# Block scale of an FP4 quantisation as a scalar_tensor_tensor with a constant column, and new slots for the jobs of a software pipeline

## The chip, the cores and the metric

One core of one Trainium2 chip. The metric is the device time of the whole program in microseconds (us), the median of three runs. "Profiled run" is one more execution, taken with the hardware profiler; its own time is given beside its span (first to last instruction).

## The reference

The input is 16 sequences of 1024 tokens, 256 wide, float32. A selective state space layer (a Mamba layer with 4 heads of 128 channels and 16 states per channel) is followed by a gated feed-forward layer whose activations and weights are quantised to FP4 and back, 16 values to a block:

```python
def fp4_quant_dequant(x):
    xb = x.reshape(shape[:-1] + (shape[-1] // 16, 16))
    scale = jnp.max(jnp.abs(xb), axis=-1, keepdims=True) / 6.0
    scale = jnp.maximum(scale, jnp.float32(1e-12))
    idx = jnp.searchsorted(_MID, jnp.abs(xb / scale))
    return (_GRID[idx] * jnp.sign(xb) * scale).reshape(shape)

# per head:  s = s * exp(d_t * A) + (d_t * u_t) * B_t ;  y_t = sum_n s[n] * C_t[n]
x = x + mamba(layernorm(x))
n = layernorm(x)
q = fp4_quant_dequant
x = x + q(silu(q(n) @ q(w_gate).T) * (q(n) @ q(w_up).T)) @ q(w_down).T
```

## The kernel before

The work is cut in two ways. A *unit* is one head of one chunk of 512 tokens: 128 units, eight to a sequence (the four heads of the early chunk, then the four of the late one). A *tile* is 128 tokens: 128 tiles as well. So one long loop over units carries one tile of the layer norm ("norm"), the preparation of one unit ("pre"), the scan of one unit ("scan") and one tile of the output projection and the feed-forward ("post"), each job of it at a different distance from the unit being scanned. A unit is cut into 16 steps, n = 0 to 15, one for each state.

**VectorE** is the backbone. In step n it first multiplies the B row of step n+1, which TensorE has spread over the partitions of a PSUM bank, with `du` (L970, "db"; not for n+1 = 1, 5, 9, 13, whose product GpSimd makes). Then comes what `between` holds for this step, then the scan of state n (L991, `tensor_tensor_scan` of 512 tokens), then what `behind` holds. In the units of a late chunk the scan starts from a carried column, in those of an early one from 0.0.

**GpSimd (POOL)** multiplies pairs of finished states with the C rows (`weigh`, L747, eight in a unit, each needs the scan of state 2p+1), makes four B products (`drive`, L738), and does the block multiplications of the quantisation (L757, L769, L786, L799), `du` (L795), the gate of y (L763) and the power -0.5 of both variances (`rstd`, L728), for which it waits for ScalarE's sum of squares of the post tile (L568). All of its operands lie in SBUF.

**ScalarE** makes the decays (L480) and evacuates and normalises; **TensorE** does all products; **SyncE** issues the DMAs of rows.

The order on each engine is written by hand as slots: `due("post", 22)` in `step` is true in step 22 mod 16 = 6, for the tile that lies 22 // 16 units back. Within one step the jobs run in the order of the code. Each job waits on semaphores for the jobs that it needs, so the slots set the order of an engine and nothing else.

**The quantisation of an activation tile** on VectorE: `block_max` (L835), `block_scale` (L838: max times 1/6, then the maximum with 1e-12), `block_recip` (L841), and after GpSimd's and ScalarE's parts `step_up` and `step_down` (L895, L898). It is done twice for each tile: for the normalised activations (`vs`, 16 blocks, input `v2`) and for the hidden ones (`hs`, 44 blocks, input `hv`). `v_norm` on GpSimd (L769) needs `block_recip(vs)`, `h_norm` (L757) needs `block_recip(hs)`, `v_quant` (L799) needs the last `step_down` of v. The weights are quantised once at the start, with `block_scale` too and with larger steps of the same kind (L871, L845, L848, L851, L854), whose operands are all in SBUF.

The order within a unit before, as far as the argument needs it (step: jobs):

- VectorE: 0: x1 (L942); 6, before the scan: gated 0, round up h 0, block_max(v); 6, behind it: round down h 0, **block_scale(v)**, y (L937), recip(v); 7: round up h 1, gated 1, round down h 1; 8: v up, output tile (L927); 9: v down; 12: block_max(h); 14: **block_scale(h)**; 15: recip(h).
- GpSimd: 0: weigh 7 of the unit before, drive 5; 1: h_norm; 3: weigh 0, rstd; 4: weigh 1, weigh 2; 6: v_norm, drive 9; 8: drive 13; 9: gate of y; 10: h_quant, du, v_quant; 11: weigh 3; 12: weigh 4; 15: drive 1, weigh 5, weigh 6.
- ScalarE from the sum over x1 (L655) to the squares (L568): decay 6, xn, fetch h 1; decays 7, 8, mid, centred v; xnt, squares of norm (L558), decay 5, table and silu gate 0, squares of post (L568).

Of the kernel before, what the change touches and what calls it, by code (L numbers as in the profile page):

```python
# [18 lines left out]
P = 128  # L19
# [120 lines left out]
def build(nc, hidden, win_t, conv_w, conv_b, xw, dtw, dt_b, a_log, dskip, wo_t, w_gate, w_up, w_down,  # L140
# [4 lines left out]
    with ExitStack() as ctx:  # L145
# [13 lines left out]
        less = sb("less", [2, P], BF16)  # L159
        minus_half = sb("minus_half", [2])  # L160
# [198 lines left out]
        def _(sp):  # L359
# [42 lines left out]
            def step(b, j, n):  # L402
                u, due = timetable(b, j, n)
                if w := due("scan", 1):
                    spread_c(w, 2)
                if w := due("scan", 4):
                    copy_b(w, 13)
# [6 lines left out]
                if w := due("scan", 4):  # L414
                    spread_c(w, 3)
                if w := due("scan", 6):
                    spread_c(w, 4)
                if w := due("scan", 6):
                    spread_c(w, 5)
# [4 lines left out]
                if w := due("scan", 12):  # L424
                    spread_c(w, 7)
                if w := due("scan", -4):
                    copy_b(w, 5)
                if w := due("scan", 2):
                    copy_b(w, 9)
                if w := due("scan", 0):  # L430
                    spread_c(w, 1)
                if t := due("post", 0):
                    wait(sp, x1_done, t.val(plus=-1))
                    sp.dma_start(xres[:, t.mod(2), :], x_tiles[t.val()]).then_inc(ld_res[t.mod(2)], 16)
                if w := due("scan", -8):
                    copy_b(w, 1)
                if w := due("scan", 11):
                    spread_c(w, 6)
                if w := due("scan", -3):
                    spread_c(w, 0)  # L440
                if t := due("post", 78):
                    sp.wait_ge(o_done, t.val(plus=1))
                    sp.dma_start(out_tiles[t.val()], ot[:, t.mod(2), :]).then_inc(ot_free[t.mod(2)], 16)

# [13 lines left out]
        def _(act):  # L458

            act.preload_act_table_set("exp_and_others")  # L460
            act.wait_ge(zeroed, 6)
# [47 lines left out]
            def step(b, j, n):  # L509
                u, due = timetable(b, j, n)  # L510
                if v := due("pre", 7):
# [11 lines left out]
                if w := due("scan", 7):  # L523
                    decay_of(w, 12)
                if w := due("scan", 7):
                    keep_carry(w, 0)
                if t := due("norm", -4):
                    act.wait_ge(sum1_done, t.val(plus=1))
                    wait(act, xn_tp, t.val(plus=-1))
                    act.activation(xn[:, t.mod(2), 0:DM], xin[:, t.mod(2), 0:DM], ACT.Identity, bias=sum1[:, 0:1],  # L530
                                   scale=-float(DM)).then_inc(centred1, 1)
                if w := due("scan", -4):
                    decay_of(w, 3)
                if t := due("post", 28):
                    act.wait_ge(v_tp, t.val(plus=1))
                    wait(act, gu_mm, t.val(4))
                    act.activation(vt[:, :, :], bank_b[:, 0:DM].rearrange("p (k t) -> p k t", k=KM),
                                   ACT.Copy).then_inc(vt_done, 1)
# [12 lines left out]
                if w := due("scan", 9):  # L551
                    decay_of(w, 14)
                if w := due("scan", -5):
                    decay_of(w, 2)
                if t := due("norm", 2):
                    act.wait_ge(centred1, t.val(plus=1))
                    wait(act, rstd_done, t.val())
                    act.activation(xin[:, t.mod(2), :], xn[:, t.mod(2), :], ACT.Square, scale=DM ** -0.5,  # L558
                                   accum_out=ve[:, 0, 0:1]).then_inc(var1_done, 1)
                if w := due("scan", 2):  # L560
                    decay_of(w, 5)
                if t := due("post", 34):
                    silu_gate(t, 0)
                if t := due("post", 18):
                    act.wait_ge(centred2, t.val(plus=1))
                    act.wait_ge(var1_done, min(t.val(plus=12), TILES))
                    act.wait_ge(rstd_done, t.val(plus=11))
                    act.activation(xin[:, (t.val() + 1) % 2, :], v2_eps[:, :], ACT.Square, scale=DM ** -0.5,  # L568
                                   accum_out=ve[:, 1, 0:1]).then_inc(var2_done, 1)
                if w := due("scan", -3):  # L570
                    decay_of(w, 1)
                if t := due("post", 61):
                    fetch_h(t, 0)
                if w := due("scan", 19):
                    act.wait_ge(summed, w.val(PAIRS, PAIRS))
                    wait(act, joined, w.val())
                    act.wait_ge(conv_mm, min(w.val(plus=3), UNITS))
                    act.activation(ycross, cross[:, :], ACT.Copy).then_inc(cross_taken, 1)
                if t := due("post", 51):
                    act.wait_ge(h_norm, t.val(plus=1))  # L580
                    wait(act, h_round, t.val(4))
                    act.wait_ge(cross_taken, min(t.val(plus=7), UNITS))
                    act.activation(cross[:, 0:HALF], hv[t.mod(2)][:, 0:HALF], ACT.Abs, scale=POWER).then_inc(h_abs, 1)
                if v := due("pre", 19):
                    act.wait_ge(res_mm, v.val(2, 2))
                    wait(act, b_spread, v.val(N_DVE, -N_DVE))
                    act.activation(pieces[:, v.mod(2), :], pbank[:, :], ACT.Copy).then_inc(pieces_done, 1)
                if t := due("post", 19):
                    act.wait_ge(rstd_done, t.val(plus=12))
                    act.activation(v2, v2, ACT.Copy, scale=ve[:, 1, 1:2]).then_inc(v_done, 1)  # L590
                if t := due("post", 36):
                    silu_gate(t, 1)
                if v := due("pre", 20):
                    h = v.mod(HEADS)
                    act.preload_act_table_set("softplus")
                    act.wait_ge(dt_mm, v.val(plus=1))
                    wait(act, du_done, v.val(plus=-1))
                    act.activation(delta[:, v.mod(2), :], pbank[:, :], ACT.Softplus,  # L598
                                   bias=dtb[:, h:h + 1]).then_inc(delta_done, 1)
                    act.preload_act_table_set("exp_and_others")  # L600
                if t := due("post", 22):
                    act.wait_ge(v_norm, t.val(plus=1))
                    wait(act, h_op, t.val(2))
                    act.activation(bank_b[:, 0:DM], v2, ACT.Abs, scale=POWER).then_inc(v_abs, 1)
                if w := due("scan", 6):
                    decay_of(w, 11)
                if w := due("scan", 6):
                    decay_of(w, 9)
                if w := due("scan", 10):
                    decay_of(w, 15)  # L610
                if w := due("scan", -6):
                    decay_of(w, 0)
                if t := due("norm", -6):
                    act.wait_ge(ld_x[t.mod(2)], t.div(2, 16, 16))
                    wait(act, centred1, t.val())
                    x = xin[:, t.mod(2), 0:DM]
                    act.activation(x, x, ACT.Copy, accum_out=sum1[:, :]).then_inc(sum1_done, 1)
                if w := due("scan", 10):
                    decay_of(w, 13)
                if w := due("scan", 1):  # L620
                    decay_of(w, 7)
                if w := due("scan", 1):
                    decay_of(w, 8)
                if v := due("pre", 17):
                    act.wait_ge(res_mm, v.val(2, 1))
                    act.activation(mid[:, :], pbank[:, :], ACT.Copy).then_inc(mid_done, 1)
                if t := due("post", 17):
                    act.wait_ge(sum2_done, t.val(plus=1))
                    wait(act, v_tp, t.val())
                    act.activation(v2, x1[:, t.mod(4), :], ACT.Identity, bias=sum2[:, 0:1],  # L630
                                   scale=-float(DM)).then_inc(centred2, 1)
                if t := due("norm", 17):
                    act.wait_ge(xn_tp, t.val(plus=1))
                    wait(act, z_mm, t.div(4, 4, -4))
                    i = t.mod(4)
# [741 lines left out]
```

## Time and profile before

| | |
|---|---|
| median of 3 runs | 4576.72 us (4568.63 to 4577.6) |
| profiled run, its own time | 4559.53 us |
| its span | 4557.4 us |
| granted TensorE clock, mean | 0.98 |
| busy share PE, DVE, ACT, POOL | 89%, 97%, 80%, 87% |

The table is the head of the profile page. It is read together with the views grouped by line and with stretches of the timeline, because one unit repeats with little change: eight units of a sequence make a period of their own. A duration in the timeline reaches a little beyond the start of the next instruction of the engine; where a sequence of instructions is added up, the distance from start to start is used.

### The profile page before, as it was taken

The numbers are of one execution on the slowest core, as the hardware profiler recorded it, in microseconds if no ns is written. First come the engines' busy times: TensorE is split into PE (matmuls) and PEld (weight loads), VectorE is DVE, ScalarE is ACT, GpSimd is POOL, SyncE is SP. The second block draws the span as 40 slices with busy tenths as digits, with TensorE's granted clock in tenths as the row PEclk, the third lists the DMA queues.
The fourth block names the chain that finished last, engine by engine and source line by source line (L and its number), as shares of the span: only waits on it lengthen the run. The fifth ranks groups of instructions, "written<-read, shape, count | busy, mean of one in ns | idle before, by whom it ended". The sixth has DMA issues, their size and how long they took to land. (4 is left out here: it accounts for less than half of the span.)

```text
span 4557.4 us, 64901 instructions
## 1 busy us (share of the span) xinstructions
PE 4062.7 (89%) x18397; PEld 1949.4 (43%) x18732; DVE 4430.2 (97%) x5804; ACT 3647.9 (80%) x6807; POOL 3945.2 (87%) x2461
## 2 busy tenths in 40 slices
PE   5889899998999989899898888989899899898987
PEld 2234444444444444444444444444444444444444
DVE  7999999999999999999999999999999999999995
ACT  5888788887888878788787888878788788787874
POOL 6989898898988889888898888989889898888984
PEclk8999999999999999999999999999999999999999
DMA  4645455454544545444454454545445454554541
GB/s 122 206 166 175 164 164 172 161 169 164 168 160 166 170 165 168 166 162 164 163 175 163 153 169 164 168 159 177 157 162 177 158 168 164 166 167 158 175 160 34
DMA packets 288970, 739.07 MB, mean 162 GB/s; under 512 B 35686, under 2 KB 87014, under 8 KB 288614
## 3 DMA queue, kind: packets, MB, share of 16 engines
q1 hardware_dynamic: 286912, 732.75, 48.2%
q8 instruction: 152, 2.49, 0.2%
q10 hardware_dynamic: 1702, 2.16, 0.2%
q14 instruction: 204, 1.67, 0.1%
HBM read 709.61 MB, written 25.17 MB: 161 GB/s over the span
## 5 line engine op out<-in xcount | busy, mean ns | idle before, releaser
L747 POOL TENSOR_TENSOR prod<-state,cs 128x1024 f32<-128x1024 f32 x1024 | 2395.7, 2359 | 140.2 <-DVE state L991 138.5
L970 DVE TENSOR_TENSOR db<-db,du 128x512 f32<-128x512 f32 x1536 | 1036.9, 675 | 42.9 <-PE db L1035 28.5
L1050 PE MATMUL ybank<-prod,ident 64*64 64x512 f32 x4096 | 1047.1, 632 | 7.7 <-DVE state L991 6.1
L480 ACT ACTIVATE decay<-delta,aneg 128x512 f32<-128x512 f32 x1536 | 1049.2, 712 | 4.6 <-DVE state L991 2.4
L1050 PE MATMUL cross<-prod,ident 64*64 64x512 f32 x4096 | 1047.0, 632 | 0.0
L991 DVE TENSOR_TENSOR_SCAN state<-decay,carry,db 128x512 f32<-128x512 f32 x768 | 952.8, 1254 | 0.0
L991 DVE TENSOR_TENSOR_SCAN state<-decay,db 128x512 f32<-128x512 f32 x768 | 908.5, 1196 | 7.9 <-PE bank_b L1298 7.9
L1035 PE MATMUL db<-pieces,sel 128*128 128x512 bf16 x1242 | 486.2, 391 | 334.5 <-DVE state L991 332.7
L738 POOL TENSOR_TENSOR brow<-brow,du 128x512 f32<-128x512 f32 x512 | 646.3, 1273 | 0.0
L1035 PEld LDWEIGHTS db<-pieces,sel 128*128 128x128 bf16 x1536 | 147.8, 96 | 1164.5 <-DVE state L991 838.3
L480 ACT ACTIVATE db<-delta,aneg 128x512 f32<-128x512 f32 x512 | 350.7, 685 | 202.2 <-DVE state L991 202.2
L1050 PEld LDWEIGHTS ybank<-prod,ident 64*64 64x64 f32 x4096 | 253.9, 138 | 460.6 <-issue 402.5
L1122 PE MATMUL bank_a<-wd,ht 128*128 128x256 f32 x1536 | 373.7, 380 | 37.4 <-DVE state L991 36.3
L1107 PE MATMUL bank_a<-wg,vt 128*128 128x352 f32 x1024 | 358.3, 472 | 2.7 <-ACT hh L497 1.6
L1074 PE MATMUL bank_b<-wu,vt 128*128 128x352 f32 x1024 | 344.7, 459 | 4.2
L728 POOL TENSOR_TENSOR ve<-ve,minus_half 128x2 f32<-128x2 f32 (+1 forms) x139 | 97.8, 704 | 281.8 <-ACT xin L568 274.1
L1122 PEld LDWEIGHTS bank_a<-wd,ht 128*128 128x128 f32 x1536 | 294.0, 192 | 90.1 <-issue 56.4
L991 DVE TENSOR_TENSOR_SCAN state<-db,carry,brow 128x512 f32<-128x512 f32 x256 | 324.5, 1268 | 0.0
L991 DVE TENSOR_TENSOR_SCAN state<-db,brow 128x512 f32<-128x512 f32 x256 | 308.6, 1206 | 0.0
L1137 PE MATMUL bank_a<-wo,yg 128*128 128x256 f32 x1024 | 263.5, 380 | 16.2 <-DVE state L991 11.4
L1148 PE MATMUL pbank<-xnt,win 128*128 128x512 f32 x512 | 270.5, 614 | 5.6 <-ACT delta L598 5.1
L1148 PE MATMUL bank_a<-xnt,win 128*128 128x512 f32 x512 | 261.8, 593 | 8.8 <-issue 6.5
(132 smaller groups left out, 7570.0 us busy)
## 6 DMA issues: line engine op xcount, KB each, us to landing
cs<-c_rows SPq DMA_DIRECT2D x1024, 512.0 KB, 4.3
brow<-b_rows SPq DMA_DIRECT2D x512, 256.0 KB, 3.3
xin<-in_hidden SPq DMA_DIRECT2D x128, 128.0 KB, 3.7
xres<-in_hidden SPq DMA_DIRECT2D x128, 128.0 KB, 4.5
out_x<-ot SPq DMA_DIRECT2D x128, 128.0 KB, 4.0
c_rows<-xdbl SPq DMA_DIRECT2D x128, 32.0 KB, 2.9
b_rows<-xdbl SPq DMA_DIRECT2D x128, 32.0 KB, 2.6
win<-in_win_t SPq DMA_DIRECT2D x1, 1024.0 KB, 5.0
```

Of the source, the lines that this page charges most:

```text
L480: act.activation(out, delta[:, w.mod(2), :], ACT.Exp, scale=aneg[:, w.mod(HEADS), n:n + 1]).then_inc(done, 1)
L738: pool.tensor_tensor(brow[:, s, :], brow[:, s, :], du[:, w.mod(2), :], ALU.mult).then_inc(db_pool, 1)
L747: pool.tensor_tensor(prod[:, r, :, :], state[:, 2 * p:2 * p + 2, :], cs[:, c, :, :], ALU.mult).then_inc(weighted, 1)
L970: dve.tensor_tensor(t[:, :], t[:, :], du[:, gu % 2, :], ALU.mult).then_inc(db_done, 1)
L991: dve.tensor_tensor_scan(state[:, n, :], by, plus, start, ALU.mult, ALU.add).then_inc(scanned, 1)
L1035: pe.matmul(db[g % DB_BANKS][:, :], sel[:, gn, :], pieces[:, gu % 2, :], start=True, stop=True).then_inc(b_spread, 1)
L1050: last = pe.matmul((ybank, cross)[k][c * Q:(c + 1) * Q, :], ident[rows, rows], prod[rows, p % P_RING, k, :], start=(p == 0), stop=(k == 1 ...
L1074: last = pe.matmul(bank_b[:, 0:HALF], vt[:, k, :], wu[:, k, part * HALF:(part + 1) * HALF], start=(k == 0), stop=(k == KM - 1))
L1107: last = pe.matmul(bank_a[:, 0:HALF], vt[:, k, :], wg[:, k, part * HALF:(part + 1) * HALF], start=(k == 0), stop=(k == KM - 1))
L1122: last = pe.matmul(bank_a[:, 0:DM], ht[:, k, :], wd[:, k, :], start=(k == 0), stop=(k == KI - 1))
L1137: last = pe.matmul(bank_a[:, 0:DM], yg[:, t.mod(8) // 4, h, i * P:(i + 1) * P], wo[:, h, :], start=(h == 0), stop=(h == HEADS - 1))
L1148: return pe.matmul((pbank, bank_a)[part][:, :], win[:, k, part * DI + h * P:part * DI + (h + 1) * P], xnt[:, v.mod(8) // 4, k, :], start=( ...
```

## The change

`block_scale` is written with another instruction. Its second operand becomes a tensor: a column of 1e-12 in SBUF, read with step 0 along the blocks. A memset fills the column at the start, and the five waits on that stage count one more.

```diff
+        least = sb("least", [1])
...
+            pool.memset(least[:, :], SCALE_MIN).then_inc(zeroed, 1)
...
             def block_scale(s):
-                return dve.tensor_scalar(s[:, 1, :], s[:, 0, :], 1.0 / 6.0, SCALE_MIN, ALU.mult, ALU.max)
+                return dve.scalar_tensor_tensor(s[:, 1, :], s[:, 0, :], 1.0 / 6.0,
+                                                least[0:s.shape[0], :].broadcast_to([s.shape[0], s.shape[2]]),
+                                                ALU.mult, ALU.max)
```

And all five engines get new slots; no job is added or taken away. In the order of the new code, a unit is:

- VectorE: 5, behind the scan: gated 0, round up h 0; 6, behind: round down h 0, block_max(v), y; 7, before the scan: **block_scale(v)**; 7, behind: recip(v), round up h 1, gated 1; 9, before: round down h 1; 9, behind: v up; 10: v down; 11, before: output tile; 12: block_max(h); 14: **block_scale(h)**; 15: x1, recip(h).
- GpSimd: 0: weigh 6 of the unit before; 1: weigh 7 of it, drive 5; 2: h_norm; 3: weigh 0, rstd; 4: drive 9; 5: weigh 1, weigh 2; 6: v_norm, gate of y; 8: weigh 3; 9: drive 13; 11: v_quant, h_quant, du; 12: weigh 4; 13: drive 1; 14: weigh 5.
- ScalarE from the sum over x1 to the squares of post: centred v, xn, decays 6, 7; fetch h 1; decay 8, mid, squares of norm; carry, decay 5, xnt, decay 10, table and silu gate 0; evacuation of `cross` (L578), squares of post.
- TensorE: among others the gate product (L1107) now stands ahead of the last sum_up and of the spread of B row 6, and the up product behind that.
- SyncE: the rows of C and B are fetched at other steps, 0 to 2 steps later or earlier for most.

The core of the diff on VectorE and GpSimd:

```diff
             def between(b, j, n, due):
-                if t := due("post", 38):
-                    gated(t, 0)
-                if t := due("post", 54):
-                    round_up_h(t, 0)
-                if t := due("post", 22):
...
-                    block_max(v2, vs).then_inc(v_scale, 1)
+                if t := due("post", 23):
+                    dve.wait_ge(v_scale, t.val(3, 1))
+                    block_scale(vs).then_inc(v_scale, 1)
+                if t := due("post", 57):
+                    round_down_h(t, 1)
+                if t := due("post", 75):
...
             def behind(b, j, n, due):
...
-                if t := due("post", 22):
-                    dve.wait_ge(v_scale, t.val(3, 1))
-                    block_scale(vs).then_inc(v_scale, 1)
...
+                if t := due("post", 46):
+                    dve.wait_ge(h_scale, t.val(3, 1))
+                    block_scale(hs).then_inc(h_scale, 1)
...
@@ gpsimd, step @@
+                if w := due("scan", 12):
+                    weigh(w, 4)
...
+                if w := due("scan", -3):
+                    drive(w, 1)
...
+                if w := due("scan", 14):
                     weigh(w, 5)
...
+                if w := due("scan", 5):
                     weigh(w, 1)
                 if w := due("scan", 4):
+                    drive(w, 9)
...
+                if w := due("scan", 5):
                     weigh(w, 2)
...
+                if w := due("scan", 3):
+                    weigh(w, 0)
+                t1, t2 = due("norm", 3), due("post", 19)
+                if t1 or t2:
+                    rstd(t1, t2)
```

## Rows read from the trace of the kernel before

**Rows 1.** Page: busy time of each engine, share of the span, instructions.
```profile
PE 4062.7 (89%) x18397; PEld 1949.4 (43%) x18732; DVE 4430.2 (97%) x5804; ACT 3647.9 (80%) x6807; POOL 3945.2 (87%) x2461
```
**Rows 2.** Windows, eight units: length, busy of PE, PEld, DVE, ACT, POOL.
```profile
1203.21:1479.00 275.79, 252.12 (x1144) 120.98 (x1164) 272.63 (x361) 225.94 (x424) 243.47 (x153) 0.98 0.50 166
```
**Rows 3.** Groups by line, DVE, whole span: count | busy us, mean ns | idle.
```profile
L991 DVE TENSOR_TENSOR_SCAN state<-decay,db 128x512 f32<-128x512 f32 x768 | 908.5, 1196 | 7.9 <-PE bank_b L1298 7.9
...
L838 DVE TENSOR_SCALAR hs<-hs 128x44 f32<-128x44 f32 x128 | 171.2, 1338 | 0.2
L838 DVE TENSOR_SCALAR vs<-vs 128x16 f32<-128x16 f32 x128 | 170.5, 1332 | 0.0
```
**Rows 4.** Timeline, DVE, block_scale(h) of two early units in a row.
```profile
2035.38 0.27 DVE L838 TENSOR_SCALAR hs<-hs 128x44 f32<-128x44 f32 x1
...
2068.42 0.28 DVE L838 TENSOR_SCALAR hs<-hs 128x44 f32<-128x44 f32 x1
```
**Rows 5.** Timeline, DVE, a unit of a late chunk.
```profile
1293.83 0.39 DVE L898 SCALAR_TENSOR_TENSOR v_eps<-bank_b,hw 128x256 f32<-128x256 bf16 x1
...
1301.44 0.67 DVE L970 TENSOR_TENSOR db<-db,du 128x512 f32<-128x512 f32 x1
1302.02 1.26 DVE L991 TENSOR_TENSOR_SCAN state<-decay,carry,db 128x512 f32<-128x512 f32 x1
1303.21 2.24 DVE L838 TENSOR_SCALAR hs<-hs 128x44 f32<-128x44 f32 x1
...
1315.99 0.70 DVE L970 TENSOR_TENSOR db<-db,du 128x512 f32<-128x512 f32 x1 [0.54 <-remote]
...
1321.17 1.05 DVE L838 TENSOR_SCALAR vs<-vs 128x16 f32<-128x16 f32 x1
1322.13 0.73 DVE L937 SCALAR_TENSOR_TENSOR yg<-uu,dsk,ybank 128x512 f32<-128x512 f32 x1
...
1329.62 0.39 DVE L898 SCALAR_TENSOR_TENSOR v_eps<-bank_b,hw 128x256 f32<-128x256 bf16 x1
```
**Rows 6.** Timeline, POOL, the same unit; in brackets the idle before.
```profile
1294.30 0.62 POOL L799 TENSOR_TENSOR v_eps<-v_eps,vs 128x256 f32<-128x256 f32 x1
...
1299.51 1.27 POOL L738 TENSOR_TENSOR brow<-brow,du 128x512 f32<-128x512 f32 x1
1300.74 4.66 POOL L747 TENSOR_TENSOR prod<-state,cs 128x1024 f32<-128x1024 f32 x2
...
1316.87 0.69 POOL L728 TENSOR_TENSOR ve<-ve,minus_half 128x2 f32<-128x2 f32 x1 [2.30 <-ACT xin L568]
1317.52 4.66 POOL L747 TENSOR_TENSOR prod<-state,cs 128x1024 f32<-128x1024 f32 x2
```
**Rows 7.** Timeline, DVE, quantisation of the weights: start us, duration us.
```profile
30.82 2.22 DVE L871 SCALAR_TENSOR_TENSOR state<-state 88x2048 f32<-88x2048 f32 x1
...
66.43 2.58 DVE L851 TENSOR_TENSOR yg<-yg 128x1408 f32<-128x1408 f32 x1
```
**Rows 8.** Timeline, POOL, the same stretch.
```profile
30.98 4.50 POOL L814 TENSOR_TENSOR yg<-yg,prod 128x1408 f32<-128x1408 f32 x1 [0.37 <-DVE prod L841]
...
65.85 1.68 POOL L795 TENSOR_TENSOR du<-delta,uu 128x512 f32<-128x512 f32 x1
70.75 2.58 POOL L814 TENSOR_TENSOR yg<-yg,prod 128x1408 f32<-128x1408 f32 x1 [3.22 <-DVE yg L854]
```
**Rows 9.** Groups by line, POOL: count | busy us, mean ns | idle.
```profile
L786 POOL TENSOR_TENSOR hh<-hh,hs 128x704 f32<-128x704 f32 x128 | 177.9, 1390 | 13.7 <-DVE hh L898 13.7
```
**Rows 10.** Timeline, ACT, from the sum over x1 to the squares.
```profile
1308.99 0.42 ACT L655 ACTIVATE x<-x 128x256 f32<-128x256 f32 x1 [3.00 <-DVE x L942]
...
1310.79 1.33 ACT L480 ACTIVATE decay<-delta,aneg 128x512 f32<-128x512 f32 x2
...
1315.78 0.46 ACT L497 ACTIVATE hh<-bank_a 128x352 f32<-128x352 f32 x1 [0.24 <-PE bank_a L1107]
1316.14 0.41 ACT L568 ACTIVATE xin<-v_eps 128x257 f32<-128x257 f32 x1
```

More of the change, by code:

```diff
@@ L512, in step @@
+                if due("post", 37) and not due("pre", 21):
+                    act.preload_act_table_set("exp_and_others")
+                if w := due("scan", 6):
+                    decay_of(w, 9)
+                if v := due("pre", 6):
                     h = v.mod(HEADS)
@@ L532, in step @@
[L532 to L538, printed above, removed]
+                if t := due("post", 65):
+                    fetch_h(t, 1)
+                if w := due("scan", -3):
+                    decay_of(w, 4)
@@ L570, in step @@
[L570 to L583, printed above, removed]
@@ L618, in step @@
[L618 to L631, printed above, removed]
@@ L667, in step @@
-                if due("post", 37) and not due("pre", 21):
-                    act.preload_act_table_set("exp_and_others")
-                if w := due("scan", 5):
-                    decay_of(w, 10)
+                if t := due("post", 28):
+                    act.wait_ge(v_tp, t.val(plus=1))
+                    wait(act, gu_mm, t.val(4))
+                    act.activation(vt[:, :, :], bank_b[:, 0:DM].rearrange("p (k t) -> p k t", k=KM),
+                                   ACT.Copy).then_inc(vt_done, 1)
@@ L672, in unit @@
+                if w := due("scan", -4):
+                    decay_of(w, 3)
             def unit(trip, j):
@@ L1247, in side @@
                     last.then_inc(xn_tp, 1)
-                if w := due("scan", 8):
-                    sum_up(w, (1,))
-                if w := due("scan", 8):
-                    spread_b(w.val(NST, 11))
+                if t := due("post", 34):
+                    gate(t, 0, (0, 1))
+                if t := due("post", 70):
+                    down(t, (0, 1))
+                if v := due("pre", 6):
+                    pe.wait_ge(xnt_done, v.div(4, 4, 4))
+                    wait(pe, delta_done, v.val())
+                    in_proj(v, 0, 0)
@@ new lines, in side @@
+                if v := due("pre", 6):
+                    in_proj(v, 0, 1).then_inc(x_mm, 1)
+                if t := due("post", 70):
+                    down(t, (2, 3))
+                if w := due("scan", 6):
+                    spread_b(w.val(NST, 10))
+                if v := due("pre", 6):
+                    conv_tap(v, (0, 1))
+                if w := due("scan", 16):
+                    sum_up(w, (4,))
+                if t := due("post", 29):
+                    pe.wait_ge(v_quant, t.val(plus=1))
+                    if peeled and t.val() == 0:
+                        pe.wait_ge(xnt_done, 11)
+                    else:
+                        wait(pe, h_op, t.val(2))
+                    for k in range(KM):
+                        last = pe.transpose(bank_b[:, k * P:(k + 1) * P], v2_eps[:, k * P:(k + 1) * P], ident[:, :])
+                    last.then_inc(v_tp, 1)
@@ L1273, in unit @@
+                if w := due("scan", 4):
+                    spread_b(w.val(NST, 7))
+                if t := due("post", 36):
+                    gate(t, 1, (0, 1))
             def unit(trip, j):
```

508 lines of the change are left out of this document (246 added, 262 removed).

## The prediction

> **What bounds the kernel now.** I read the page first: VectorE is busy 97% of the span, TensorE 89%, GpSimd 87% [rows 1]. Then the windows over eight units, one sequence: VectorE is busy 272.63 of 275.79 us, so it idles 0.39 us in a unit of 34.5 us, and TensorE follows with 31.5 us a unit [rows 2]. VectorE's instruction stream is the bound, and what shortens it shortens the program, down to some 31.5 us a unit, where TensorE stands.
>
> Then the groups by line. `block_scale` works on 44 or 16 elements and takes 1338 and 1332 ns on average, 341.7 us in all or 2.67 us a unit [rows 3]; one in an early unit takes 0.27 us [rows 4]. Why is in two timelines side by side. block_scale(h) starts at 1303.21 and ends at 1305.45 [rows 5]; GpSimd's pair of weighs started at 1300.74 and ended at 1305.40 [rows 6]. block_scale(v) starts at 1321.17 and ends at 1322.22; the pair from 1317.52 ended at 1322.18. So a `tensor_scalar` stands still until GpSimd's running instruction is over and ends 0.05 us later. What it costs is the rest of a weigh (2.35 us each, 4.66 the pair), that is, a matter of phase: 0.27 us in early units, 2.24 in late ones for h.
>
> **The change: the instruction.** Does the new form still wait? It has two inputs in SBUF, and the start of this trace has three such forms. L871, a scalar_tensor_tensor on two SBUF inputs, runs 30.82 to 33.04, and GpSimd's L814, started at 30.98, takes 4.50 us, where the same shape takes 2.58 with VectorE on PSUM work [rows 7, 8]: 1.92 us longer, about the 2.06 that L871 still had to go. The other way round L851, an add of two SBUF tensors, starts at 66.43 while `du` runs until 67.53, and takes 2.58 us, on 1408 elements, where L871 takes 2.22 on 2048, so some 1.55 on as many [rows 7, 8]: 1.0 more, nearly the 1.10 that `du` still ran. So a form with two SBUF inputs waits as a whole for GpSimd and GpSimd for it. No row shows one with 16 or 44 elements, or an input of step 0; the wait came before the first element in the large ones, so I take it that size changes nothing.
>
> The Trainium skill has the rule: SBUF — State Buffer, section "Who interferes with whom", says that a Vector instruction with two SBUF inputs contends with a GpSimd instruction that reads SBUF, since its second input comes through the shared read interface. It speaks against this change, the rows at the start agree, and by it the substitution alone gains nothing; the section's other case, at most one SBUF input and no 2-port mode, would free the 2.67 us, but this instruction is not of that kind.
>
> Its own length without a wait is between nothing more than now (0.27 us with 44 elements, [rows 4]) and 0.39 us, a scalar_tensor_tensor on 256 elements [rows 5]. I take no change; at the upper end 0.1 x 2 x 128 = 26 us. The memset of the column and the larger counts lie in the first microseconds: nothing.
>
> **The change: the slots.** With the wait kept, the time hangs on where the two block_scales meet GpSimd. I lay out one late unit of the new order, taking each stretch of before and adding or taking off what has moved. Distances start to start: scan 1.19, db 0.58 [rows 5], drive 1.23 [rows 6] and `du` the same, its shape being the same; from durations less an overlap of 0.04 to 0.07: y 0.66 and output tile 0.33, of the size of v down [rows 5], v_quant 0.58 [rows 6], h_quant 1.35 [rows 9].
>
> 1. *v down to block_scale(h).* Before: 1303.21 - 1293.83 = 9.38 [rows 5]. The step down moves from step 9 to 10 (less one db and one scan, 1.77), the output tile comes in between (0.33): 7.94. GpSimd starts v_quant 0.47 after the start of v down (1294.30, [rows 6]), for it waits for it; then come h_quant, du, weigh 4, drive 1, weigh 5: 0.47 + 0.58 + 1.35 + 1.23 + 2.31 + 1.23 + 2.35 = 9.52. So block_scale(h) meets weigh 5 and takes 9.57 - 7.94 = 1.63 us. In an early unit each scan is 0.06 shorter (1.196 against 1.26, [rows 3, 5]; five of them here), and it takes 1.93. The same sum for before gives weigh 5 over at 9.3 and block_scale(h) at 9.08 early and 9.38 late: 0.27 in the one, and in the other the next weigh, 2.24, as the rows have it.
> 2. *End of block_scale(h), called E, to block_scale(v).* Before: 1321.17 - 1305.45 = 15.72, with 0.54 of idle [rows 5]. y and one db move ahead of it (1.24). The idle was VectorE waiting for B row 6, whose spread stood behind the gate product on TensorE; it now stands behind a gate product that runs earlier, so I let it go. 15.72 - 0.54 + 1.24 = 16.42; early 15.95.
> 3. *Where GpSimd is then.* rstd waits for ScalarE's squares (2.30 us idle, [rows 6]). From the sum over x1 to the squares it was 1316.14 - 1308.99 = 7.15 [rows 10]. Now x1 stands in step 15, and the sum starts at E + 2.15. In the stretch decay 10 (0.61, half of the two in 1.33 less the overlap, [rows 10]), the evacuation of cross (0.55) and a carry (0.12) are added, about 0.5 of waits (for the sum, and of decay 5 for scan 2), and the 0.24 of the gate wait goes: 8.7. rstd starts 0.73 after the squares (1316.87 - 1316.14): R = E + 11.6, early 11.5. Then rstd 0.65, drive 9 1.23, weighs 1 and 2 4.66: weigh 1 is over at R + 4.23 = 15.8, weigh 2 at R + 6.54 = 18.1. block_scale(v) at 16.42 meets weigh 2 and takes 1.8 us; early, at 15.95, 2.1.
> 4. *End of block_scale(v) to v down.* Before 1329.62 - 1322.13 = 7.49 [rows 5]; less y, a db and the output tile, plus a db and a scan: 7.69, early 7.45.
>
> Sum, late: 16.42 + 1.8 - 0.09 + 7.69 + 7.94 + 1.63 = 35.4. Early: 15.95 + 2.1 - 0.09 + 7.45 + 7.64 + 1.93 = 35.0. Four of each: 281.5 us. Before: 275.8 for eight units [rows 2], of which an early one takes 33.04 (2068.42 - 2035.38, [rows 4]) and so a late one 35.9. The late units gain their idle and 0.6 us of wait; the early ones lose the good phase of block_scale(h). +5.5 us in eight units, 16 sequences: +88 us. On the profiled run 4559.5 + 88 = 4648 (span 4557.4, 2.1 outside it); the median of the runs lay 17 us above the profiled one, so 4665 as a median. I take 4655.
>
> The other moves cost nothing by this layout. GpSimd is ready for v_quant about 1.3 us before v down is, which covers the later v_norm; were that cover gone, all of it would be added to block_scale(h), up to a weigh. gated 0 has some 1 us over the up product and the silu, round up h 0 some 0.4 us over ScalarE's magnitude: this is the thinnest cover, and what is missing there falls on VectorE in full (0.3 us a unit would be 38 us). SyncE's rows have a microsecond or more at each moved fetch, by the order of waits.
>
> **Rivals.** *A: the new form does not wait.* A tiny instruction or one with a step-0 input might slip past. Then 2.67 us a unit shrink to some 0.4, the idle goes, and the stream is 31.9 us a unit; TensorE's 31.5 [rows 2] is then next, with 0.4 to 1 us of new waits. 32.3 to 32.9 a unit against 34.5 is 205 to 280 us less: about 4280 to 4355, say 4320. Against it speak [rows 7, 8]. Chance 0.16.
>
> *B: the phase falls on the other side of an edge.* block_scale(v) meets weigh 1 and not weigh 2 if rstd starts later than R = 11.7 in early units, 12.2 in late ones; my R is 11.5 and 11.6 with perhaps 0.6 of doubt. Between the edges the early ones wait 0.3 and the late ones 2.2: 4 x 33.2 + 4 x 35.8 = 276, the time of now, 4570 (chance 0.20, half of it within 0.2%). Beyond both, 4 x 33.7 + 4 x 34.0 = 271: 80 us less, 4490 (chance 0.14). So a later GpSimd is faster here, and it decides in a few tenths of a microsecond.
>
> *The forecast itself*: 0.50, from 4590 (R a microsecond earlier) to 4700 (block_scale(h) at its full 2.3 us, or TensorE and ScalarE late by 0.3 us).
>
> **Numbers.** What a measurement here can tell from no change is about 0.2%. Slower: 0.50 + 0.05 of B = 0.55. Same: 0.10. Faster: 0.16 of A, 0.14 and 0.05 of B = 0.35. The range 4460 to 4705 takes in the forecast and B and leaves out A and a little above: 0.81.
>
> **What would show it.** Step by step: L838's place taken by scalar_tensor_tensor groups with a mean well over 1 us for both shapes, each ending 0.05 us behind a GpSimd instruction; means near 0.2 would prove A. block_scale(h) 1.6 late and 1.9 early, ending with weigh 5; block_scale(v) about 2, ending with weigh 2, rstd at E + 11.6. An early unit of 35.0 and a late one of 35.4. DVE's idle waits near nothing; a wait of L895 for ScalarE or of L905 for TensorE of some tenths would show the thin cover broken. The prediction falls if the form does not wait, or if weigh 1 is the one that is met.

## The result and the profile after

The change makes the program slower: 4644.8 us (4643.5 to 4648.9) against 4577.2 (4568.6 to 4580.9), a ratio of 1.0152 with a 95% interval of 1.0134 to 1.0170. The profiled run took 4644.8 us, 85.2 more than the profiled run of before; the forecast's sum gave 88 more, 4648, and its final figure, as a median, was 4655.

The head of the page of after:

```profile
span 4642.6 us, 64922 instructions
...
PE 4048.4 (87%) x18417; PEld 1960.1 (42%) x18732; DVE 4511.5 (97%) x5804; ACT 3707.2 (80%) x6807; POOL 3949.6 (85%) x2462
```

TensorE's busy time changes by 14 us and GpSimd's by 4; ScalarE's grows by 59, but it stands idle for a fifth of the span in both kernels [rows 1]. VectorE, busy 97% in both, has the same 5804 instructions and is busy 81.3 us longer. The groups by line of VectorE (count | busy us, mean ns | idle before) say in which of them:

```profile
L974 DVE TENSOR_TENSOR db<-db,du 128x512 f32<-128x512 f32 x1536 | 1040.3, 677 | 53.9 <-PE db L1039 30.4 <-remote 22.9
...
L840 DVE SCALAR_TENSOR_TENSOR hs<-hs,least 128x44 f32<-128x44 f32 x128 | 216.3, 1690 | 0.2
L840 DVE SCALAR_TENSOR_TENSOR vs<-vs,least 128x16 f32<-128x16 f32 x128 | 215.4, 1683 | 0.1
```

The two groups of `block_scale` went from 341.7 us [rows 3] to 431.7: +90.0. All other instructions together are 8.7 shorter, and the idle time (span less busy) went from 127.2 to 131.1: +3.9. 90.0 - 8.7 + 3.9 = 85.2, the whole of the difference.

The windows over eight whole units at the same place in the sequence, before and after (length, then busy us of PE, PEld, DVE, ACT, POOL, the granted clock of TensorE, DMA):

```profile
1203.58:1480.09 276.51, 252.84 (x1149) 121.60 (x1169) 273.35 (x361) 226.59 (x424) 244.19 (x153) 0.98 0.50 166
```

```profile
1231.32:1514.22 282.90, 250.79 (x1152) 122.02 (x1168) 279.86 (x361) 230.63 (x424) 244.38 (x153) 0.98 0.49 162
```

The window of [rows 2], 275.79 us, was cut 0.7 us shorter than the eight units are.

Now an early unit in the timelines (start us, duration us; in brackets the idle before), first VectorE, from one block_scale(h) to the next and on to the next block_scale(v), with y (L937) ahead of that:

```profile
1231.32 1.89 DVE L840 SCALAR_TENSOR_TENSOR hs<-hs,least 128x44 f32<-128x44 f32 x1
...
1249.12 2.08 DVE L840 SCALAR_TENSOR_TENSOR vs<-vs,least 128x16 f32<-128x16 f32 x1
...
1258.51 0.39 DVE L904 SCALAR_TENSOR_TENSOR v_eps<-bank_b,hw 128x256 f32<-128x256 bf16 x1
...
1266.20 1.89 DVE L840 SCALAR_TENSOR_TENSOR hs<-hs,least 128x44 f32<-128x44 f32 x1
...
1282.73 0.73 DVE L937 SCALAR_TENSOR_TENSOR yg<-uu,dsk,ybank 128x512 f32<-128x512 f32 x1
...
1283.99 2.08 DVE L840 SCALAR_TENSOR_TENSOR vs<-vs,least 128x16 f32<-128x16 f32 x1
```

then GpSimd around the last block_scale(h) and block_scale(v):

```profile
1265.66 4.68 POOL L749 TENSOR_TENSOR prod<-state,cs 128x1024 f32<-128x1024 f32 x2
...
1279.49 0.69 POOL L730 TENSOR_TENSOR ve<-ve,minus_half 128x2 f32<-128x2 f32 x1 [0.61 <-ACT xin L547]
1280.14 1.27 POOL L740 TENSOR_TENSOR brow<-brow,du 128x512 f32<-128x512 f32 x1
1281.37 4.67 POOL L749 TENSOR_TENSOR prod<-state,cs 128x1024 f32<-128x1024 f32 x2
```

The pair of weighs from 1281.37 is over at 1286.04, block_scale(v) at 1286.07. The first weigh of the pair of 1265.66 is over at about 1268.0, block_scale(h) at 1268.09. So both `block_scale`s of an early unit now stand behind a weigh, where before block_scale(h) slipped through in 0.27 us and only block_scale(v) waited (1.69 us in most early units), and the early unit takes 1266.20 - 1231.32 = 34.88 us where it took 33.04 [rows 4].

### The profile page after: what moved, and what is told of

Its sections match the earlier page's. It is cut to its first block and busy times, and to the rows that moved or that the text cites. A ratio compares the mean times of both kernels' runs of the same rounds, so it can differ in the third digit from the quotient of the medians.

```text
span 4642.6 us, 64922 instructions
## 1 busy us (share of the span) xinstructions
PE 4048.4 (87%) x18417; PEld 1960.1 (42%) x18732; DVE 4511.5 (97%) x5804; ACT 3707.2 (80%) x6807; POOL 3949.6 (85%) x2462
## 5 line engine op out<-in xcount | busy, mean ns | idle before, releaser
L974 DVE TENSOR_TENSOR db<-db,du 128x512 f32<-128x512 f32 x1536 | 1040.3, 677 | 53.9 <-PE db L1039 30.4
L481 ACT ACTIVATE decay<-delta,aneg 128x512 f32<-128x512 f32 x1536 | 1038.7, 709 | 0.1
L1054 PEld LDWEIGHTS ybank<-prod,ident 64*64 64x64 f32 x4096 | 264.6, 138 | 585.6 <-issue 556.2
L1126 PE MATMUL bank_a<-wd,ht 128*128 128x256 f32 x1536 | 393.7, 381 | 1.2 <-ACT ht L506 1.2
L1111 PE MATMUL bank_a<-wg,vt 128*128 128x352 f32 x1024 | 345.7, 460 | 0.9 <-issue 0.4
L1054 PEld LDWEIGHTS cross<-prod,ident 64*64 64x64 f32 x4096 | 254.3, 138 | 0.0
```

Source lines behind the costliest of these rows:

```text
L481: act.activation(out, delta[:, w.mod(2), :], ACT.Exp, scale=aneg[:, w.mod(HEADS), n:n + 1]).then_inc(done, 1)
L974: dve.tensor_tensor(t[:, :], t[:, :], du[:, gu % 2, :], ALU.mult).then_inc(db_done, 1)
L1054: last = pe.matmul((ybank, cross)[k][c * Q:(c + 1) * Q, :], ident[rows, rows], prod[rows, p % P_RING, k, :], start=(p == 0), stop=(k == 1 ...
L1111: last = pe.matmul(bank_a[:, 0:HALF], vt[:, k, :], wg[:, k, part * HALF:(part + 1) * HALF], start=(k == 0), stop=(k == KM - 1))
L1126: last = pe.matmul(bank_a[:, 0:DM], ht[:, k, :], wd[:, k, :], start=(k == 0), stop=(k == KI - 1))
```

## Experiments

**The two halves of the change.** One kernel is before with the new form alone, the other is after with the old form in its place:

```diff
 # e1_form_only: old slots
-                return dve.tensor_scalar(s[:, 1, :], s[:, 0, :], 1.0 / 6.0, SCALE_MIN, ALU.mult, ALU.max)
+                return dve.scalar_tensor_tensor(s[:, 1, :], s[:, 0, :], 1.0 / 6.0, least..., ALU.mult, ALU.max)
 # e2_slots_only: new slots
-                return dve.scalar_tensor_tensor(s[:, 1, :], s[:, 0, :], 1.0 / 6.0, least..., ALU.mult, ALU.max)
+                return dve.tensor_scalar(s[:, 1, :], s[:, 0, :], 1.0 / 6.0, SCALE_MIN, ALU.mult, ALU.max)
```

Each ratio below is that to runs of before made beside it; their medians lay between 4567.7 and 4582.4 us.

> The kernel before with the new form of block_scale alone, all slots as before. My theory (a form with two SBUF inputs waits for GpSimd's running instruction just as the tensor_scalar does, and is as short without a wait): the same time within 0.3%, 4565 to 4590 us, block_scale means near 1.34 us for both shapes, 0.3 us in early units and 2.2 in late ones for the hidden tile. Rival (the new form holds or waits longer than the old one, and the slots are not what made the kernel slower): 4600 us or more. Rival (the form is free, and the new slots ate the gain): about 4300 us.

Measured: 4568.4 us, ratio 0.9968 (0.9956 to 0.9980).

> The kernel after with the old tensor_scalar put back, new slots kept. My theory (the slots alone made it slower): 4635 to 4655 us, block_scale means near 1.69 us. Rival (the form costs): near 4577 us, as before.

Measured: 4643.7 us, ratio 1.0143 (1.0126 to 1.0160). The groups of `block_scale` in the two, first of the new form in the old slots:

```profile
L840 DVE SCALAR_TENSOR_TENSOR hs<-hs,least 128x44 f32<-128x44 f32 x128 | 175.6, 1372 | 0.2
```

```profile
L840 DVE TENSOR_SCALAR vs<-vs 128x16 f32<-128x16 f32 x128 | 216.3, 1690 | 0.1
L840 DVE TENSOR_SCALAR hs<-hs 128x44 f32<-128x44 f32 x128 | 214.3, 1674 | 0.2
```

For 44 elements the mean in the old slots is 1372 ns by the new form and 1338 by the old [rows 3]; in the new ones it is 1690 by the new form and 1674 by the old. The form waits as the old one does, and the slots carry the whole loss. The 0.3% by which the form alone came out faster has no row that explains it: its `block_scale`s take 5 us more than before, not less, and its profiled run (4570.2 us) was 10.7 us longer than that of before. It is not read as an effect of the form.

**What the wait is worth.** The same instruction with one input in SBUF and the other in PSUM (a bank of B products that is being read around it anyway; the second operation passes the first result on, so the maximum with 1e-12 is left out), in the new slots and in the old:

```diff
-                return dve.scalar_tensor_tensor(s[:, 1, :], s[:, 0, :], 1.0 / 6.0, least..., ALU.mult, ALU.max)
+                return dve.scalar_tensor_tensor(s[:, 1, :], s[:, 0, :], 1.0 / 6.0,
+                                                db[g % DB_BANKS][:, 0:s.shape[2]], ALU.mult, ALU.bypass)
```

> The kernel after, with a block_scale of the activations that reads one input from SBUF and one from a PSUM bank, the second one being bypassed: it leaves out the maximum with 1e-12. My theory (only a second input in SBUF or the two-port form waits for GpSimd): block_scale takes 0.2 to 0.3 us, VectorE's stream is 31.9 us a unit, and TensorE (31.5 us busy a unit before) and new waits hold it at 32.0 to 32.9: 4240 to 4360 us. Rival (TensorE or the loop through ScalarE bounds at once, and the waits for GpSimd cost nothing on the path): above 4500 us.

Measured: 4220.8 us, ratio 0.9219 (0.9205 to 0.9233).

> The kernel before, old slots, with the same block_scale from one SBUF and one PSUM input, without the maximum with 1e-12. My theory: 2.67 us a unit of wait shrink to 0.4; the old slots had no cover planned for it, so more new waits than in the new slots: 4250 to 4400 us. If the new slots were laid out for a stream without the wait, they are faster than these here by up to 2%; if they are plainly worse, slower here too.

Measured: 4222.0 us, ratio 0.9222 (0.9208 to 0.9236). Both came out below the ranges expected. The groups and the head of the page in the new slots:

```profile
L847 DVE SCALAR_TENSOR_TENSOR hs<-hs,db 128x44 f32<-128x44 f32 x128 | 21.7, 169 | 0.2
L847 DVE SCALAR_TENSOR_TENSOR vs<-vs,db 128x16 f32<-128x16 f32 x128 | 19.8, 155 | 0.1
```

```profile
PE 3963.2 (94%) x18417; PEld 1941.6 (46%) x18732; DVE 4121.0 (98%) x5804; ACT 3682.2 (87%) x6807; POOL 3946.7 (94%) x2462
```

0.16 us each in place of 1.69: 390 us of waiting are gone from VectorE (431.7 - 41.5), and 424 from the program. The other 34 are idle time: VectorE waits 44.6 us less ahead of its B products (9.3 in place of 53.9), for a reason that is told in point 4 below, and 11 us more for ScalarE's magnitudes. Which slots are used then makes no difference (1.2 us): they matter only through the wait. The Trainium skill, SBUF — State Buffer, section "Who interferes with whom", says that a Vector instruction with at most one SBUF input and no 2-port mode does not contend with GpSimd, and that one with two contends with a GpSimd instruction that reads SBUF; at 16 and 44 elements the traces agree with both, 0.155 and 0.169 us by the one and 1.683 and 1.690 by the other.

These kernels change two things at once: the second input lies in PSUM, and its operation is bypassed. The timeline of after shows that PSUM is enough. y (L937, at 1282.73) is the same instruction with both operations in use, one tensor input in SBUF (`uu`) and one in PSUM (`ybank`); it starts and ends inside the pair of weighs that runs from 1281.37 to 1286.04, and takes 0.73 us, its mean over the whole program. Whether a bypassed second input in SBUF would be free too was not tried.

**The same with nothing left out.** The floor moves ahead of the factor, max(6e-12, m) and then times 1/6, each as one such instruction:

```diff
+                dve.scalar_tensor_tensor(s[:, 0, :], s[:, 0, :], 6.0 * SCALE_MIN, other, ALU.max, ALU.bypass)
+                dve.scalar_tensor_tensor(s[:, 1, :], s[:, 0, :], 1.0 / 6.0, other, ALU.mult, ALU.bypass)
```

> New slots, block_scale of the activations as two instructions that each read one input from SBUF and a bypassed one from a PSUM bank: the maximum with 6e-12, then times 1/6; nothing of the computation is left out. By the run with one such instruction (4221 us, 0.16 us each and below 0.1 us from start to start) a second costs 0.1 to 0.2 us twice in a unit: 4235 to 4275 us. Rival (the added wait between the two is longer, or TensorE's 94% hides the second one): 4300 us, or 4221 us.

Measured: 4270.4 us, ratio 0.9354 (0.9333 to 0.9375).

> The same exact form in the old slots: 4235 to 4275 us, within 0.3% of the new slots, as the two were with the single instruction (4221 and 4222 us).

Measured: 4273.2 us, ratio 0.9361 (0.9336 to 0.9385). This beats both kernels, before by 6.4% and after by 8%. It costs 50 us over the version without the floor: 256 more instructions, 0.19 to 0.20 us each. Again the slots make no difference.

**Block scales on ScalarE.** It takes them off VectorE altogether; the 1e-12 is added as a bias in place of the maximum:

```diff
+                    act.activation(vs[:, 1, :], vs[:, 0, :], ACT.Identity, bias=least[:, 0:1],
+                                   scale=1.0 / 6.0).then_inc(v_scale, 1)
```

> The kernel after, with the block scales of the activations made by ScalarE (max times 1/6 plus 1e-12, in place of the maximum with 1e-12) instead of VectorE; the weights' keep their form. My theory: VectorE loses both waits and both instructions, and ScalarE gains two of about 0.2 us; if ScalarE comes in time (block_scale(v) is wanted about 1.8 us after the maximum, block_scale(h) about 3.5), 4190 to 4240 us, a little below the 4221 of the form that reads PSUM. Rival (ScalarE, 87% busy in that run, comes late and VectorE waits for it): 4260 to 4400 us.

Measured: 4510.5 us, ratio 0.9854 (0.9835 to 0.9872).

> The same move to ScalarE in the kernel before, old slots. My theory: 4190 to 4250 us; here ScalarE waited 2 us in front of the magnitudes of v, where the scale of v now goes. Rival as in the new slots: 4260 to 4400 us.

Measured: 4492.0 us, ratio 0.9812 (0.9794 to 0.9830). Both missed the numbers of both of their theories. VectorE's group of the reciprocal of v, in the old slots, tells why:

```profile
L851 DVE RECIPROCAL vs<-vs 128x16 f32<-128x16 f32 x128 | 32.3, 253 | 281.2 <-ACT vs L608 281.2
```

VectorE idles 2.2 us on average ahead of this reciprocal (281.2 us in 128 units; 258.8 in the new slots), waiting for a 0.3 us instruction of ScalarE that has its place between decays. The wait for GpSimd became a wait for ScalarE's queue: less work on VectorE (4111 us busy in place of 4430 before), and most of the gain given back.

**The phase.** The forecast rests on the claim that the loss is a matter of where `block_scale` meets a weigh. If so, a *later* GpSimd must be faster once weigh 1, and not weigh 2, is the one that is met: in the early unit above weigh 1 is over at about 1283.7, 0.3 us before block_scale(v) begins. First rstd was moved by a filler on ScalarE ahead of the squares:

```diff
+                    act.activation(idle_out[:, 0:48], least[:, 0:1].broadcast_to([P, 48]), ACT.Copy)   # or 0:256
                     act.activation(xin..., v2_eps[:, :], ACT.Square ...)
```

> The kernel after, with one more ScalarE instruction (a copy of 48 elements into a scratch tile, some 0.16 us) right ahead of the squares for which GpSimd's rstd waits. In the trace of after rstd starts 11.4 us behind the end of block_scale(h) in early units; by my layout block_scale(v) goes on meeting weigh 2 as long as that stays below 11.67, and then each tenth is added to the wait. My theory: a little slower than after, 4650 to 4680 us, block_scale(v) of early units about 2.2 us. Rival (the time hangs on VectorE's own stream and an added ScalarE instruction with idle time behind it costs nothing): 4645 us.

Measured: 4665.0 us, ratio 1.0193 (1.0171 to 1.0214), as the theory had it: rstd starts 11.53 us behind the end of block_scale(h), not yet at the edge, and block_scale(v) takes 2.21 us in an early unit in place of 2.08.

> The kernel after, with a ScalarE copy of 256 elements (some 0.4 us) ahead of the squares. rstd then starts at 11.8 in early units, beyond the edge of 11.67, and near 12.1 to 12.5 in late ones, about at their edge of 12.1 to 12.2. My theory: block_scale(v) of early units meets weigh 1 at its end and takes 0.1 to 0.4 us in place of 2.1, so that an early unit takes about 33.1 us; late units are the same or better by a flip: more work on ScalarE makes the program faster, 4470 to 4560 us. Rival (a later rstd only delays): 4645 us or more, up to 4700.

Measured: 4688.2 us, ratio 1.0242 (1.0224 to 1.0261): a miss, and inside the range of the rival. The trace says why the number alone does not decide. The filler also held up ScalarE's magnitude, and with it VectorE's step up, so that block_scale(v) came later too, 16.03 behind the end of block_scale(h) in place of 15.90. rstd stood at 11.70, and the edge was now at 11.80 (16.03 less the 4.23 from rstd to the end of weigh 1). In one late unit both fell right. VectorE there, and GpSimd's pair of weighs ran from 1369.26:

```profile
1371.53 0.16 DVE L842 SCALAR_TENSOR_TENSOR vs<-vs,least 128x16 f32<-128x16 f32 x1
```

0.16 us, by the kernel's own two-input form: it slipped in where weigh 1 of the pair ended, at about 1371.6, and that unit took 33.7 us where its kind takes 35.6.

Then the weighs alone were moved, by a filler on GpSimd behind rstd, a product and then a power:

```diff
                 pool.tensor_tensor(ve[:, which, 1], ve[:, which, 0], minus_half[:, which], ALU.pow)
+                pool.tensor_tensor(idle_out[:, :], minus_half[:, :], minus_half[:, :], ALU.mult)   # e9_weighs_later
+                pool.tensor_tensor(idle_out[:, :], least[:, 0:1]..., minus_half[:, :], ALU.pow)   # e12_weighs_later_pow
```

> The kernel after, with one more small GpSimd instruction (128 x 2 elements, some 0.65 us) behind every rstd, so that drive 9 and weighs 1 and 2 come that much later and nothing on ScalarE moves. In the run with the larger ScalarE delay rstd came only 0.3 us later and VectorE's round up h 0 with it, so that the edge was not passed. My theory: weigh 1 is now over at about 16.3 us behind the end of block_scale(h), after block_scale(v) is due at 15.9, so it waits for weigh 1 (about 0.4 us) and not weigh 2 (2.08): an early unit goes from 34.9 to about 33.2 us, half of the late ones from 35.4 to 33.7 and the others get 0.65 longer. 4480 to 4540 us: more work on GpSimd makes the program some 3% faster than after. Rival (what follows on GpSimd is on the path, so that its added 0.65 us a unit is lost): 4645 to 4730 us.

Measured: 4668.8 us, ratio 1.0226 (1.0204 to 1.0249), a miss, and inside the range of the rival. GpSimd's rows:

```profile
1217.32 0.69 POOL L733 TENSOR_TENSOR ve<-ve,minus_half 128x2 f32<-128x2 f32 x1 [1.93 <-ACT xin L550]
1217.97 0.20 POOL L737 TENSOR_TENSOR idle_out<-minus_half 128x2 f32<-128x2 f32 x1
```

The product moved the weighs by 0.15 us, not by the 0.65 that I had taken from rstd, which is as small but a power: too little to pass the edge, and block_scale(v) grew by 0.15.

> The kernel after with one more GpSimd instruction behind rstd, now a power on 128 x 2 elements like rstd itself, whose next instruction starts 0.65 us later (the product tried before took 0.15). Its result is used by nobody, so nothing of the computation changes; GpSimd only works longer. Theory (the loss is a matter of phase): in an early unit of the kernel after, weigh 1 is over about 15.7 us behind the end of block_scale(h), and block_scale(v) comes at 15.90 and waits for weigh 2, 2.08 us. With 0.65 more, weigh 1 is over at 16.3, block_scale(v) meets weigh 1 and takes about 0.4 us, the early unit falls from 34.9 to 33.2 us, and more work on GpSimd makes the program faster than both the kernel before and the kernel after: 4420 to 4540 us, L840 on vs with a mean under 1000 ns. Rival (more work on an engine that is 85% busy, beside a VectorE that waits for it, only costs): block_scale(v) stays over 2 us and grows by the delay, 4645 to 4760 us.

Measured: 4548.2 us, ratio 0.9940 (0.9920 to 0.9961). More work on GpSimd, whose result nobody uses, made the kernel after 97 us *faster*, and 0.6% faster than before. The size is 8 us outside the range I gave. The groups, and VectorE in three units, early, late and late:

```profile
L846 DVE SCALAR_TENSOR_TENSOR hs<-hs,least 128x44 f32<-128x44 f32 x128 | 217.6, 1700 | 0.2
L846 DVE SCALAR_TENSOR_TENSOR vs<-vs,least 128x16 f32<-128x16 f32 x128 | 118.8, 928 | 0.1
```

```profile
1255.04 1.89 DVE L846 SCALAR_TENSOR_TENSOR hs<-hs,least 128x44 f32<-128x44 f32 x1
...
1272.82 0.43 DVE L846 SCALAR_TENSOR_TENSOR vs<-vs,least 128x16 f32<-128x16 f32 x1
...
1288.25 1.90 DVE L846 SCALAR_TENSOR_TENSOR hs<-hs,least 128x44 f32<-128x44 f32 x1
...
1340.11 0.18 DVE L846 SCALAR_TENSOR_TENSOR vs<-vs,least 128x16 f32<-128x16 f32 x1
...
1365.46 0.70 DVE L980 TENSOR_TENSOR db<-db,du 128x512 f32<-128x512 f32 x1 [0.96 <-PE db L1045]
...
1374.83 1.97 DVE L846 SCALAR_TENSOR_TENSOR vs<-vs,least 128x16 f32<-128x16 f32 x1
```

block_scale(h), which the filler does not touch, keeps its mean (1700 ns against 1690); block_scale(v) fell from 215.4 to 118.8 us in all, and these 96.6 us are the whole gain. The early unit takes 1288.25 - 1255.04 = 33.2 us, the number of the theory. It isn't more because the edge isn't passed in every unit: in six of the eight from 1218.82 on block_scale(v) takes 0.18 to 0.44 us, in two it takes 1.97 and 2.21. Those two are the ones in which VectorE idled about a microsecond for a B row (1.11 and 0.96 us, the second in the bracket at 1365.46), so that it reached block_scale(v) when weigh 1 was over, and met weigh 2. In both TensorE ran at a lowered clock just before: 0.57 granted over 1224 to 1228 and over 1361 to 1365, 1.00 over 1258 to 1262 in the unit without the idle (point 4 below).

## Why the prediction was right, point by point

1. *The form waits.* Right, by both tests: 1690 and 1683 ns in after, and 1372 ns in place of 1338 in the old slots. That size and a step-0 input change nothing was an assumption of the forecast; it held. Its own length was put between 0 and 0.1 us over the old form's, and the sum took 0. The means in the slots hold the wait and cannot tell. Where no wait is seen, in the weights at the start, it takes 287 ns on 88 x 128 elements and the old form 224; the shortest on 128 x 16 are 0.16 us by either.
2. *The layout.* Each interval of the sum, forecast first and measured second. Early unit: v down to block_scale(h) 7.64, 1266.20 - 1258.51 = 7.69; block_scale(h) 1.93, 1.89; E to block_scale(v) 15.95, 15.90; rstd E + 11.5, + 11.40; block_scale(v) 2.1, 2.08; from its end to v down 7.45, 7.32; the unit 35.0, 34.88. Late unit (VectorE's block_scale(h) at 1337.18 and 1372.79): v down to block_scale(h) 7.94, 7.94; block_scale(h) 1.63, 1.65; E to block_scale(v) 16.42, 16.34; rstd E + 11.6, + 11.89, so that weigh 2 ends later; block_scale(v) 1.8, 2.13; then 7.69, 7.55; the unit 35.4, 35.61. Eight units: 281.5, 282.90.
3. *The sum: partly luck.* The mechanism is right, and the late unit came out 0.2 too short and the early one 0.1 too long. That the total of 88 us meets 85.2 rests on errors that cancel. By the sum's own figures the eight units grow by 281.5 - 275.8 = 5.7 us and not by 5.5 (91 us in all). The window gives 282.90 - 276.51 = 6.4, which would be 102. Over 14 stretches of eight units one after the other, measured from block_scale(h) to block_scale(h), the means are 277.2 us before and 282.5 after, 5.4 apart: in before four of them took 278.4 to 283.9, the last 273.0 and the others about 276. So the base of the forecast was 1.4 too low and its sum 1.0 too low. Besides, the profiled run of before (4559.5) was faster than every other run beside it, and that of after was not: by medians the change is 67.6 us (4644.8 - 4577.2). The 17 us that the forecast added to come from a profiled run to a median did not appear in after, whose two agree (4644.8).
4. *The idle time on a B row: wrong.* The forecast let 0.54 us in a late unit go, because the spread of row 6 would stand behind earlier work. But VectorE idles 53.9 us ahead of its B products after and 42.9 before. What failed is the cause that it gave to the wait, TensorE's order alone. It has no term for TensorE's clock, and the rows show that this is what the wait comes with. Here are the same steps of two late units of after, whose block_scale(h) stand at 1301.08 and 1372.79. Granted clock of TensorE (third number from the end), the first at half of its full speed, that is 1.2 and not 2.4 GHz:

```profile
1308.00:1310.00 2.00, 2.00 (x12) 0.27 (x4) 1.99 (x3) 1.69 (x6) 2.00 (x2) 0.50 0.24 86
1379.00:1381.00 2.00, 2.00 (x20) 0.79 (x13) 2.00 (x3) 2.00 (x6) 2.00 (x2) 1.00 0.18 68
```

TensorE's last sums of C-weighted states and the spread of B row 4 behind them, in the first unit, then VectorE; and TensorE in the second:

```profile
1308.49 1.07 PE L1054 MATMUL ybank<-prod,ident 64*64 64x512 f32 x2
...
1309.35 1.07 PE L1054 MATMUL ybank<-prod,ident 64*64 64x512 f32 x2
...
1310.37 0.58 PE L1039 MATMUL db<-pieces,sel 128*128 128x512 bf16 x1
...
1310.99 0.70 DVE L974 TENSOR_TENSOR db<-db,du 128x512 f32<-128x512 f32 x1 [1.01 <-PE db L1039]
```

```profile
1379.47 0.60 PE L1054 MATMUL ybank<-prod,ident 64*64 64x512 f32 x2
...
1379.90 0.59 PE L1054 MATMUL ybank<-prod,ident 64*64 64x512 f32 x2
...
1380.44 0.39 PE L1039 MATMUL db<-pieces,sel 128*128 128x512 bf16 x1
```

The order is the same in both. A group of sums takes 0.86 us from start to start at the lower clock and 0.43 at the full one, so the spread starts 9.29 us behind the start of block_scale(h) in the one unit (1310.37 - 1301.08) and 7.65 in the other (1380.44 - 1372.79), where VectorE does not wait. The late unit of [rows 5] is such a case too: TensorE's clock there is 0.50 over 1308 to 1310, and the 0.54 us of idle follow, up to 1315.99; at 1381 to 1383, in a late unit of before without such an idle, it is 1.00. In both units of after TensorE had been idle for 1.0 to 1.4 us, twice, waiting for VectorE's scans, before the stretch shown, so these rows do not tell why the clock fell in one and not in the other; that stays open.

It is so throughout. Between 200 and 4350 us VectorE has 43 idles of over 0.3 us ahead of a B product in after, and 42 of them come within 5 us of a stretch at the lower clock; in before it has 62, and all come within 9 us of one. The runs as wholes agree: mean granted clock, and idle us of VectorE ahead of its B products.

| run | clock | idle |
|---|---|---|
| before | 0.980 | 42.9 |
| after | 0.978 | 53.9 |
| e7_scale_on_act_new_slots | 0.975 | 41.0 |
| e12_weighs_later_pow | 0.977 | 55.2 |
| e8_scale_on_act_old_slots | 0.992 | 4.6 |
| e3_free_new_slots | 0.994 | 9.3 |
| e4_free_old_slots | 0.994 | 3.6 |

The mistake cost the forecast little, since block_scale(v) has no fixed length. In the unit from 1408.12, whose clock falls as well, VectorE idles 0.90 us and block_scale(v) takes 1.32 us in place of 2.13; the unit takes 1443.92 - 1408.12 = 35.8 us, 0.2 to 0.5 more than its neighbours. Where the wait had been nearly removed it costs more, as in the two units of the last experiment.

5. *The thin cover*, 0.4 us of round up h 0 over ScalarE's magnitude: it held (L901 idles 4.0 us in the whole span, 4.9 before). That it is thin was shown by the larger filler on ScalarE, 0.42 us long, which made step up and all behind it 0.13 us later (16.03 in place of 15.90).
6. *Rival A* did not occur, but its price was mis-sized. Without the wait I had put TensorE, at 31.5 us a unit, as the next bound, with 0.4 to 1 us of new waits, 4320 us. The kernels without the wait take 4221 and 4222, even less than 31.9 us a unit without any new wait would give: 4577 - 128 x (34.5 - 31.9) = 4244. TensorE is then busy 94% of the span and VectorE 98%, and VectorE idles only 9.3 us on B rows where it idled 53.9. TensorE's 31.5 us was no bound for a unit of 31.9, and it was no fixed number either: with the granted clock at 0.994 in place of 0.980 it is busy 3963.2 us in all and not 4062.7 [rows 1]. Whether its clock holds because VectorE no longer makes it wait is not shown.
7. *Rival B* did not occur, by a small margin: the edge lay where it was put (11.7 in early units) and rstd at 11.40, 0.3 short of it, less than the 0.6 by which the forecast doubted its own R. Its prices for the early unit (33.2) and its sign were seen when GpSimd was made later.

## What to carry to other kernels

If a small instruction has a mean many times its work, put it beside the other engine's timeline: if its end follows the end of the other's instruction, its length is a phase, and each reordering of anything ahead of it re-rolls it. Lay out one period with start-to-start distances and say which instruction is met and how far the edge is; then remove the wait by the kind of its operands (here the second input in PSUM: 6.5% with nothing left out, in either order of slots) and don't tune the slots around it. Moving the instruction to a third engine gives back most of the gain if that engine's queue has no place for it at the right time (here 1.5% and 1.9% were left). And before an idle time is put down to the order on another engine, compare the same steps in a unit with the idle and in one without it, with TensorE's granted clock beside both.

## What the runs showed that I had not expected

GpSimd takes 0.69 us for a power on 128 x 2 elements and 0.20 us for a product on as many. VectorE takes 0.155 us for a scalar_tensor_tensor on 128 x 16 elements with one input in PSUM; the two-input form in SBUF takes 0.16 to 0.18 on as many where it slips in at the end of a weigh, so on that size the form itself costs next to nothing. Short stretches at half of TensorE's clock, in a trace with a mean of 0.98, stand ahead of nearly all of VectorE's waits for B rows. And an instruction that only keeps GpSimd busy 0.65 us longer in every unit took 97 us off a program of 4645.
